# One program per engine for the value projection and the self-attention of a decoder layer

## The reference

```python
x = x + _L0_attn_ref(_layernorm(x, axis=-1), L0_attn_w_q, L0_attn_w_k, L0_attn_w_v, L0_attn_w_o)
...
def _L0_attn_ref(x, w_q, w_k, w_v, w_o):
    # HEADS = 32, D_K = 16
    q, k, v = (proj(w_q), proj(w_k), proj(w_v))
    scores = jnp.einsum('bhqd,bhkd->bhqk', q, k) / jnp.sqrt(jnp.float32(D_K))
    attn = jax.nn.softmax(scores, axis=-1)
    out = jnp.einsum('bhqk,bhkd->bhqd', attn, v)
    out = out.transpose(0, 2, 1, 3).reshape(B, S, HIDDEN)
    return jnp.einsum('bse,oe->bso', out, w_o)
```

## Time and profile before

| | before |
|---|---|
| runs | 1589.81, 1588.82, 1583.85 us; median 1588.82 |
| the profiled execution | 1588.91 us, of which the span of instructions 1587.1 us |
| TensorE busy | 1477.8 us, 93% of the span |
| VectorE, GpSimd, ScalarE busy | 1110.4 us (70%), 493.6 us (31%), 428.2 us (27%) |
| mean granted clock of TensorE | 0.968 of full speed |
| value block, first to last transfer or instruction | 203.85 to 267.95 us |
| self-attention block, first instruction | 268.21 us |

### The profile page before, as it was taken

One profiled execution on the slowest core, in us unless ns is written; L12 is line 12 of the kernel. 1 busy time (PEld: TensorE's weight loads), 2 busy tenths in 40 slices (PEclk: granted clock), 3 DMA queues, 4 the chain that ended last, 5 costly groups with the idle time before them and its releaser, 6 DMA issues. The chain is left out here.

```text
span 1587.1 us, 25598 instructions
## 1 busy us (share of the span) xinstructions
PE 1477.8 (93%) x10080; PEld 1179.6 (74%) x10080; DVE 1110.4 (70%) x1659; ACT 428.2 (27%) x738; POOL 493.6 (31%) x443
## 2 busy tenths in 40 slices
PE   6999968899998569999999999999999999998698
PEld 5788856677776457877878777877878777776476
DVE  3655432577879677887787787787878777886454
ACT  4111133445554221222221221222212212211311
POOL 4322212233333123432423433433424334231022
PEclk9999979999999789999999999999999999999799
DMA  7554311000000410020110011020011201000211
GB/s 233 168 174 160 103 40 40 1 15 21 9 1 1 146 53 15 28 67 14 40 55 27 27 54 34 21 67 27 29 53 29 66 15 41 14 27 1 91 52 55
DMA packets 79106, 83.90 MB, mean 53 GB/s; under 512 B 9824, under 2 KB 50928, under 8 KB 78736
## 3 DMA queue, kind: packets, MB, share of 16 engines
q1 hardware_dynamic: 68976, 63.42, 12.5%
q10 hardware_dynamic: 9216, 16.78, 3.2%
q0 software_dynamic: 800, 2.11, 0.5%
HBM read 59.22 MB, written 23.07 MB: 52 GB/s over the span
## 5 line engine op out<-in xcount | busy, mean ns | idle before, releaser
L1266 POOL TENSOR_TENSOR p_q_rot<-p_ra,p_rb 128x512 f32<-128x512 f32 x128 | 167.0, 1305 | 287.1 <-DVE p_rb L603 287.1
L1036 PE MATMUL p_ps_y<-p_wo_hi,p_o_hi 128*128 128x512 f32 x512 | 212.7, 416 | 5.9 <-DVE p_o_lo L1185 5.7
L75 PE MATMUL p_ps_q<-b_xt_hi,p_wq_hi 128*128 128x512 f32 x512 | 211.7, 413 | 0.0
L1037 PE MATMUL p_ps_y<-p_wo_lo,p_o_hi 128*128 128x512 f32 x512 | 203.3, 397 | 0.0
L1038 PE MATMUL p_ps_y<-p_wo_hi,p_o_lo 128*128 128x512 f32 x512 | 202.9, 396 | 0.0
L76 PE MATMUL p_ps_q<-b_xt_lo,p_wq_hi 128*128 128x512 f32 x512 | 202.7, 396 | 0.0
L77 PE MATMUL p_ps_q<-b_xt_hi,p_wq_lo 128*128 128x512 f32 x512 | 201.4, 393 | 0.0
L1258 POOL TENSOR_TENSOR p_pn<-p_p,p_inv 128x512 f32<-128x512 f32 x64 | 66.8, 1044 | 298.0 <-DVE p_inv L1165 298.0
L1195 DVE TENSOR_TENSOR x_sb<-p_ps_y,x_sb 128x512 f32<-128x512 f32 x128 | 88.1, 688 | 87.0 <-PE p_ps_y L1038 87.0
L1107 ACT ACTIVATE p_o_hi<-p_ps_o 128x512 fp32r<-128x512 f32 x128 | 69.5, 595 | 280.6 <-PE p_ps_o L1023 280.6
L601 DVE TENSOR_TENSOR p_ra<-p_ps_q,b_cos_t 128x512 f32<-128x512 f32 x128 | 86.0, 672 | 59.8 <-PE p_ps_q L77 56.4
(11 more groups left out here) (200 smaller groups left out, 3057.3 us busy)
## 6 DMA issues: line engine op xcount, KB each, us to landing
p_raw_q<-in_wq SPq DMA_DIRECT2D x36, 256.0 KB, 3.2
v_scratch<-p_v_out SPq DMA_DIRECT2D x32, 256.0 KB
k_scratch<-p_k_out SPq DMA_DIRECT2D x32, 256.0 KB, 2.1
p_k_t<-k_scratch ACTq DMA_DIRECT2D x32, 256.0 KB, 2.6
p_v_in<-v_scratch ACTq DMA_DIRECT2D x32, 256.0 KB, 2.8
p_raw_o<-in_wo SPq DMA_DIRECT2D x32, 256.0 KB, 3.5
x_sb<-in_x SPq DMA_DIRECT2D x16, 256.0 KB, 3.0
out<-p_yb SPq DMA_DIRECT2D x16, 256.0 KB, 2.0
```

The lines of the kernel that those rows point to most:

```text
L75: nc.tensor.matmul(out, lh, rh, start=(c == 0), stop=False)
L1036: nc.tensor.matmul(ps_y[t][:, :], oh, w_hi["o"][h][:, :], start=(h == 0), stop=False)
L1037: nc.tensor.matmul(ps_y[t][:, :], oh, w_lo["o"][h][:, :], start=False, stop=False)
L1266: nc.gpsimd.tensor_tensor(q_rot[:, h, :], ra[:, :], rb[:, :], ALU.add).then_inc(q_added, 1)
```

## The change

Both blocks become one, with one program per engine. The value tiles are written out (no loop) and use `xt_hi` and `xt_lo` themselves as the stationary factors; the small buffers, ScalarE's second copy and GpSimd's copies are gone. The transposes go into the two halves of `ps_y`, the value products into `ps_o` and `ps_p[0]`; the raw value weights lie where `pn` and `pt` come later, the normalised tiles where `o_hi` and `o_lo` come later, and waits are added for it. All first loads are issued by SP at once. The first weights of self-attention are split at tiles 2 to 4, and the projections and scores that stood ahead of the loop are placed between value tiles 8 to 13. The loop of units is not changed.

```diff
-def norm_and_values(nc, stack_type, norm1, xt_hi, xt_lo, v1, ident, wv_dram):
...
         s, p = m.sb("s", [P, COLS, SEQ]), m.sb("p", [P, COLS, SEQ])
+        wv_raw_at = nc.sbuf_base
         pn = [m.sb(f"pn{i}", [P, PCOLS, SEQ]) for i in range(2)]
         pt = [m.sb(f"pt{i}", [P, ROWS * PB, P]) for i in range(2)]
+        wv_raw = nc.alloc_sbuf_tensor_at("p3_wv_raw", [P, KC, HIDDEN], F32, offset=wv_raw_at)
+        wv_hi, wv_lo = (m.sb(n, [P, KC, HIDDEN], F32R) for n in ("wv_hi", "wv_lo"))
...
+        ps_t, ps_v = [ps_y[:, i, :] for i in range(2)], [ps_o, ps_p[0]]
...
         @block.sync
         def _(sp):
+            sp.dma_start(wv_raw[:, :, :], wv_dram).then_inc(w_in, 16)
             sp.dma_start(heads[:, :], heads_dram).then_inc(heads_in, 16)
...
             def project(w, it):
                 need(pe, ready[w], group_of(it) + 1)
+                need(pe, tile_lo, min((it + 1) * TPB, TILES))
...
             def turn(j):
                 need(pe, k_spread, 2)
+                need(pe, v_copied, TILES)
...
+            def turn_tile(t):
+                need(pe, xn_ready, t + 1)
+                need(pe, tile_lo, t - 1)
+                for c in range(KC):
+                    tr = nc.tensor.transpose(ps_t[t % 2][:, c * P:(c + 1) * P], xn[t % 2][:, c * P:(c + 1) * P], ident[:, :])
+                tr.then_inc(transposed, 1)
+
+            def values(t):
+                need(pe, tile_lo, t + 1)
+                need(pe, w_ready, 1)
+                need(pe, v_copied, t - 1)
+                tile = slice(t * P, (t + 1) * P)
+                product3(nc, ps_v[t % 2][:, :], [(xt_hi[:, c, tile], xt_lo[:, c, tile], wv_hi[:, c, :], wv_lo[:, c, :])
+                                                 for c in range(KC)]).then_inc(v_done, 1)
+
+            turn_tile(0)
+            for t in range(TILES):
+                if t + 1 < TILES:
+                    turn_tile(t + 1)
+                values(t)
+                if t == 8:
+                    project("q", 0)
+                if t == 9:
+                    project("k", 0)
+                if t == 10:
+                    project("q", 1)
+                if t == 11:
+                    scores(0)
+                if t == 12:
+                    project("k", 1)
+                if t == 13:
+                    scores(1)
...
+            norm1.finish_scalar(nc, act)
+            for t in range(TILES):
+                tile_parts_hi(t)
+                if t == 0:
+                    act.wait_ge(w_in, 16)
+                    nc.scalar.activation(wv_hi[:, :, :], wv_raw[:, :, :], ACT.Copy).then_inc(w_part, 1)
+                else:
+                    copy_values(t - 1)
+                if 2 <= t < 5:
+                    split_hi(act, "qko"[t - 2], 0, done["q"], 0)
+                if t == 9:
+                    act.wait_ge(heads_in, 16)
+                    spread_q(0)
+                if t == 11:
+                    spread_k(0)
+                if t == 12:
+                    spread_q(1)
+                if t == 14:
+                    exponentials(0)
+                    spread_k(1)
+            copy_values(TILES - 1)
             exponentials(1)
...
+            norm1.finish_vector(nc, dve)
+            normalise_tile(0)
+            for t in range(TILES):
+                if t + 1 < TILES:
+                    normalise_tile(t + 1)
+                tile_parts_lo(t)
+                if t == 0:
+                    dve.wait_ge(w_part, 1)
+                    nc.vector.tensor_tensor(wv_lo[:, :, :], wv_raw[:, :, :], wv_hi[:, :, :], ALU.subtract).then_inc(w_ready, 1)
+                if 2 <= t < 5:
+                    split_lo(dve, "qko"[t - 2], 0)
+                if t == 6:
+                    dve.wait_ge(zeroed, 2)
+                    move_values(0)
+                if t == 13:
+                    shift(0)
             shift(1)
             invert(0)
```

More of the change, by code:

```diff
@@ L258, in self_attention @@
-def self_attention(nc, stack_type, x, norm2, xt_hi, xt_lo, v1, ident, wq_dram, wk_dram, wo_dram, heads_dram):
+def self_attention(nc, stack_type, x, norm1, norm2, xt_hi, xt_lo, v1, ident, wv_dram, wq_dram, wk_dram, wo_dram, heads_dram):
     with stack_type() as stack:
@@ L287, in self_attention @@
         ps_y = m.ps("ps_y", (P, 2, HIDDEN))
+        ps_t, ps_v = [ps_y[:, i, :] for i in range(2)], [ps_o, ps_p[0]]
+        w_in, w_part, w_ready = m.sem("w_in"), m.sem("w_part"), m.sem("w_ready")
+        xn_ready, transposed, tile_hi, tile_lo = (m.sem(n) for n in ("xn_ready", "transposed", "tile_hi", "tile_lo"))
+        v_done, v_copied = m.sem("v_done"), m.sem("v_copied")
         raw_in = {w: m.sem(f"raw_in_{w}") for w in "qko"}
@@ L457, in outputs_hi, with tile_parts_hi, copy_values @@
                 need(act, pv_done, (it + 1) * PARTS)
+                need(act, transposed, TILES)
                 need(act, y_done, it * TPB)
                 nc.scalar.activation(o_hi[:, :], ps_o[:, :], ACT.Copy).then_inc(out_hi, 1)
[L461 to L469, removed]
+            def tile_parts_hi(t):
+                need(act, transposed, t + 1)
+                nc.scalar.activation(xt_hi[:, :, t * P:(t + 1) * P], ps_t[t % 2].rearrange("p (c n) -> p c n", c=KC), ACT.Copy).then_inc(tile_hi, 1)
+            def copy_values(t):
+                need(act, v_done, t + 1)
+                nc.scalar.activation(v1[:, t, :], ps_v[t % 2][:, :], ACT.Copy).then_inc(v_copied, 1)
+            norm1.finish_scalar(nc, act)
[19 more added lines that the diff above has]
+            copy_values(TILES - 1)
             exponentials(1)
+            need(act, w_ready, 1)
             for n in range(UNITS_ALL):
@@ L518, in move_values @@
                 need(dve, pv_done, (it - 1) * PARTS)
+                need(dve, v_copied, min((it + 1) * TPB, TILES))
                 for r in range(2):
@@ L532, in add, with normalise_tile, tile_parts_lo @@
                         norm2.collect(nc, first + t)
[L534 to L538, removed]
+            def normalise_tile(t):
+                need(dve, transposed, t - 1)
+                norm1.apply(nc, xn[t % 2][:, :], t).then_inc(xn_ready, 1)
+            def tile_parts_lo(t):
+                need(dve, tile_hi, t + 1)
+                nc.vector.tensor_tensor(xt_lo[:, :, t * P:(t + 1) * P], ps_t[t % 2].rearrange("p (c n) -> p c n", c=KC),
+                                        xt_hi[:, :, t * P:(t + 1) * P], ALU.subtract).then_inc(tile_lo, 1)
+            norm1.finish_vector(nc, dve)
[14 more added lines that the diff above has]
+                    shift(0)
             shift(1)
@@ L579, in place_values @@
                 need(pool, pv_done, (it - 1) * PARTS)
+                need(pool, v_copied, min((it + 1) * TPB, TILES))
                 need(pool, p_norm, it * PARTS)
@@ L589, in _ @@
             place_values(0)
+            need(pool, w_ready, 1)
             normalise_p(0)
```

13 lines of the change are left out of this document (5 added, 8 removed).

## The result

The changed kernel takes 1579.46 us (median of 7 runs, 1575.1 to 1581.53), the kernel before 1588.88 us (7 runs, 1583.85 to 1590.45). The ratio is 0.9945 with a 95% interval of 0.9929 to 0.9962: 8.7 us faster, between 6.0 and 11.3. The forecast was 1579.0 us, in a range of 1575.5 to 1583.0. The ratio's centre is just beyond the 0.5% that I had called the least that can be told. Its interval excludes that nothing changed, but it still holds gains between 0.4% and 0.5%, so of the two outcomes that I had kept apart, over 0.5% faster (0.69) and within 0.5% (0.27), the measurement doesn't decide.

The account below looks back on a forecast made before the run. TensorE was taken to bound the kernel, so only its idle time or slow clock could give: 1588.9 - 9.6 (path) - 0.6 (clock) + 0.3 (loads) = 1579.0 us, range 1575.5 to 1583.

Parts of the forecast that it names:

- The path between product 8 and `turn(0)`: Start of value tile 8's product to first transpose of normalised scores: 51.40 us before, 41.81 forecast, 9.59 us saved.
- the wait for the last low part: TensorE, before the last value product: a new wait of about 1.3 us for tile 15's low part.
- the wait before `turn(0)`: TensorE, before the first transpose of normalised scores: some 2.3 us in place of 5.19.
- The clock: TensorE's clock after `turn(0)`: 0.6 us gained, the middle between 0 (it falls again) and 1.4 (it holds).
- The loads: SP's queue: heads and three weight pieces issued behind the value weights cost 0.3 us, between bounds 0 and 2.6.
- What was costed at nothing: Dropped ScalarE and GpSimd copies, splits at tiles 2 to 4, written-out loops, moved clearing and added waits: all taken as 0.
- GpSimd's clearing: Clearing of `v_x` moves to the first block's head, waits for nothing and nothing waits for it: cost 0.
- Late weights: Rival: the three loads share the rate with the value weights, costing 2.6 us in place of 0.3: 1581.3 us; chance 0.12.
- A dearer first exponential: Rival: something hidden behind ScalarE's table load comes onto the path, up to 1.05 us: 1580.0 us; chance 0.07.
- A worse phase of the loop: Rival: TensorE waits in each of 32 units; 0.3 us each ends the gain, 0.6 gives 1597.6 us; chance 0.05.
- Late tiles one by one: Rival: value products at tiles 12 to 14 also held up, 1.3 us each, 3.9 less gained: 1582.9 us; chance 0.08.
- my signs of failure: First value matmul after 215, last tiles' waits adding up to over 3.6 us, or loop units taking longer than before.

Follow-up runs that it names:

- the run without the interleaving: Changed kernel, but the four projections and two rounds of scores stand behind the last value product again; 1579.34 us, ratio 0.9951 to the kernel before.
- the run with late splits: On top of the run without the interleaving, the first self-attention weights are split behind the last value tile too; 1584.34 us, ratio 0.9979.
- the last run: Changed kernel with insertions one value tile earlier, tile 14's high part ahead of the first exponentials, and the value products' two PSUM buffers exchanged; 1573.97 us, ratio 0.9922.

## Why the prediction was right

**The path between product 8 and `turn(0)`.** 41.81 us forecast, 41.90 measured; 9.59 saved forecast, 9.50 measured. Its parts: the wait for the last low part 1.3 forecast, 0.94 measured; the wait before `turn(0)` 2.3 forecast, 1.96 measured, and 0.34 more between `turn(0)` and `turn(1)`. The first is shorter because TensorE's own work was laid out too short: value product 13 ended 31.39 us behind the start of product 8 and not 31.01, and product 14 ended 0.55 us later than laid out (a few hundredths at each switch between products, projections and scores, and 3.05 us for product 14 in place of 2.87), while the low part was 0.2 us late. It didn't matter, since ScalarE's and VectorE's chain set `turn(0)`: from VectorE's second maximum to `turn(0)` 5.15 us were taken from before, 5.16 measured (281.27 to 286.43). That ScalarE's order makes the first and through it part of the second is shown by putting the high part first and by taking the table load away, each of which takes the first wait away.

**The clock.** Taken 0.6 between 0 and 1.4; measured 1.40, all in the first unit: from `turn(0)` to `turn(2)` 6.23 us (286.43 to 292.66), and 7.61 in the run without the interleaving. This is the term of the sum that was off: the value taken was the middle between two cases, and an execution has one or the other. At this place the clock held in all five executions with a wait of 1.4 to 1.96 us before `turn(0)` (the changed kernel and four experiments) and fell in all three with one of 5.2 us, so 1.40 was no accident of the one execution. That a wait of some two microseconds can still go either way is shown elsewhere: after 1.93 us in the run with late splits it fell, and after the 2.65 us at the loop's end it held in seven executions and fell in three.

**The loads.** Taken 0.3, measured 0: the weights took 6.00 us to land, and 6.07 before. The rule that the prediction cites from the Trainium skill (DMA: Bandwidth & Descriptors, Queues, rings and completion order) gave 0. The trace agrees with it: `heads`, issued right behind the value weights, landed 0.1 us behind them, and without them in front after 1.6 us in place of 5.7.

**What was costed at nothing.** ScalarE's second copy: shown free in the merged block. The splits at tiles 2 to 4: no wait of TensorE there; tile 3's low part was done 0.5 us ahead of its product (227.87, 228.36), where I had found 0.3. GpSimd's clearing: off the path, though not without effect (below).

**The sum.** 9.5 + 1.4 + 0.35 ahead of product 8 gives 11.25 for the stage, where I had 9.9. The 0.35 is chance of the clock in the first value product (5.07 against 5.56 us), less the slower pace. The medians moved by 9.4, the ratio says 8.7 with 2.7 either way. The span, which moved by 8.9, hides 2.60 us of the 11.25 in the scatter of the first stage. So the forecast of the whole was closer than its parts deserve, and that is luck: they were 1.3 us too small in this profile, and the scatter covers it.

**The rivals.** Late weights: out, 1.22 us of idle time against 1.24. A dearer first exponential: out, it started 0.01 us behind the table load. A worse phase of the loop: out, from `turn(2)` on the stage takes what it took. Late tiles one by one: out, one wait and no others.

**The signs.** By its letter one of my signs of failure came true: TensorE's first value matmul came after 215, at 216.83. The mark was ill chosen, as it was an absolute time and the stage ahead of it scatters by 5 us; counted from the block's start it came after 10.38 us, and 10.36 before. The waits of the last tiles added up to 3.24 us, under the 3.6 that I allowed, and `turn(0)` lay at 283.8 on the old time scale, where I had 284.1.

## What to carry to other kernels

When two stages that are each bound by TensorE are merged, look at the seam first: the first weights of the next stage, loaded and split while the last tiles run. Here that was 7.6 us of the 11.25. For the filling of the next pipeline, look at what stands in the other engines' queues between its steps; here a high part ahead of the exponentials, the filling one tile earlier and a PSUM buffer not shared with `turn(0)` brought `turn(0)` 2.7 us further forward (77.31 us behind the block's start in the last run, against 79.98). Compare such edits stage by stage between fixed marks of the trace, since a change of 0.2% is lost in the scatter of an unrelated stage.

## What the hardware showed that I had not expected

- The granted clock after waits of nearly the same length: 1.00 after 1.96 us in the changed kernel, 0.51 from 270 to 272 after a wait of 1.93 us in the run with late splits. The second cost 1.7 us on a projection. One and the same wait, 2.65 us at the loop's end, had the clock at 1.00 behind it in seven executions and at 0.50 in three.
- VectorE's addition of 128 x 16 elements took 0.61 us (207.71) while GpSimd's clearing of `v_x` ran (206.45 to 208.29), and 0.17 before, where GpSimd was idle. It ended at 208.32, just behind the clearing, and in all nine executions of merged kernels it took 0.61 or 0.62 us. TensorE's wait for the first normalised tile grew by it, from 6.9 to 7.3 us, and the wait for the value weights behind it shrank from 5.8 to 5.4, so it cost no time. That the clearing is the cause is not tested.
- Three pieces of 256 KB ahead of a transfer of 1 MB in SP's queue delayed its landing by 0.43 us behind its own issue, while SP's four issues ahead of it took 2.52 us. Behind the 1 MB, 2 KB took 5.7 us to land; ahead of it, 1.6.
